# Reordering the chunk steps of a fused RWKV and expert-routing layer: the shared down projection moves one step later

## The reference

```python
# RWKV block, on layernorm(x)
xn = layer_norm(x, ln1_g, ln1_b); xx = token_shift(xn)
k, v, r = three mixes of xn and xx, times Wk, Wv, Wr
x2 = x + (sigmoid(r) * wkv(time_decay, time_first, k, v)) @ Wo.T    # wkv: a scan over the tokens
xn2 = layer_norm(x2, ln2_g, ln2_b)
kf = square(relu(mix_k(xn2) @ Wk_ffn.T))                            # 256 -> 1024
x3 = x2 + sigmoid(mix_r(xn2) @ Wr_ffn.T) * (kf @ Wv_ffn.T)
x1 = x_input + layernorm(x3)
# FFN, on xf = layernorm(x1)
shared = (gelu(xf @ w1s) * (xf @ w2s)) @ w3s                        # every token
e = argmax(xf @ Wg)
routed = (gelu(xf @ W1[e]) * (xf @ W2[e])) @ W3[e]                  # the token's own expert
out = x1 + layernorm(shared + routed)
```

## Time and profile before

| | |
|---|---|
| median of 3 runs | 1040.57 us (1040.02 to 1044.66) |
| the profiled execution | 1038.19 us, span of the core 1036.5 us |
| granted TensorE clock, mean over the span | 0.976 of full speed |
| busy in the span: PE | 934.1 us (90%), 9734 matmuls |
| busy: DVE | 760.0 us (73%) |
| busy: ACT, POOL | 589.9 us (57%), 591.9 us (57%) |
| first phase | to about 700 us |
| one turn of the loop (two steps) | 78.45 us |

### The profile page before, as it was taken

How to read it: one execution, slowest core, us unless ns; L and a number is a source line. 1 busy time by engine, 2 the same in 40 slices (tenths; PEclk the granted TensorE clock), 3 DMA queues, 4 the chain that set the end, 5 groups by cost and what they waited for, 6 DMA issues and landing times.

```text
span 1036.5 us, 28181 instructions
## 1 busy us (share of the span) xinstructions
PE 934.1 (90%) x9734; PEld 834.5 (81%) x9734; DVE 760.0 (73%) x1665; ACT 589.9 (57%) x1014; POOL 591.9 (57%) x802
## 2 busy tenths in 40 slices
PE   2388899999999999999999998879999999999994
PEld 1266788788788788888888887758999999999994
DVE  6989999999999999999999986433444444444442
ACT  5477678678678687687687675423333333333331
POOL 6346577577577577577587543234454554555553
PEclk9698999999999999999999999999999999999998
DMA  6113241341341441441443134766877788485510
GB/s 233 61 52 96 111 151 58 137 155 53 129 162 47 136 162 41 142 162 41 142 162 123 56 150 161 249 231 216 266 228 241 249 269 267 146 290 184 193 55 22
DMA packets 87330, 156.26 MB, mean 151 GB/s; under 512 B 5549, under 2 KB 68142, under 8 KB 82160
## 3 DMA queue, kind: packets, MB, share of 16 engines
q1 hardware_dynamic: 35760, 72.74, 20.5%
q10 hardware_dynamic: 46960, 65.89, 19.6%
q0 software_dynamic: 4560, 16.98, 4.3%
HBM read 178.35 MB, written 50.51 MB: 221 GB/s over the span
## 4 chain that ended last, share of the span: by engine, by line
PE 46%; DVE 18%; issue 10%; POOL 9%; ACT 7%; DMA 1%; ACTq 1%; DVEq 0%; POOLq 0%
PE up L334 9%; PE up L335 9%; PE up L336 9%; PE yp L334 4%; PE yp L335 4%; PE yp L336 4%; PE yp L538 2%; PE yp L541 2%; DVE mixed L988 2%; ACT ex L699 2%; POOL inv L1448 2%; DVE gu L1181 2%; DVE er L1058 1%; DVE arena L963 1%; POOL sh_s L1529 1%
## 5 line engine op out<-in xcount | busy, mean ns | idle before, releaser
L334 PE MATMUL up<-mix_s,arena 128*128 128x128 f16 x1248 | 211.1, 219 | 1.5 <-DMA arena<-w_split 1.5
L335 PE MATMUL up<-mix_s,arena 128*128 128x128 f16 x1248 | 211.1, 219 | 0.0
L336 PE MATMUL up<-mix_s,arena 128*128 128x128 f16 x1248 | 211.1, 219 | 0.0
L1529 POOL TENSOR_TENSOR sh_s<-gu,sh_s 128x512 f16<-128x512 f32 x64 | 84.1, 1316 | 141.5 <-ACT sh_s L762 141.5
L334 PE MATMUL up<-xf_s,arena 128*128 128x256 f16 x512 | 139.5, 272 | 1.1 <-DVE gu L1181 1.1
L336 PE MATMUL up<-xf_s,arena 128*128 128x256 f16 x512 | 139.5, 273 | 0.0
L335 PE MATMUL up<-xf_s,arena 128*128 128x256 f16 x512 | 139.5, 272 | 0.0
L1634 POOL TENSOR_TENSOR kf_s<-ex,kf_s 128x512 f16<-128x512 f32 x78 | 90.2, 1157 | 85.4 <-ACT kf_s L922 85.3
L1401 DVE SCALAR_TENSOR_TENSOR ex<-up,ex 128x512 f32<-128x512 f32 x78 | 54.0, 692 | 101.6 <-ACT ex L916 101.2
L334 PEld LDWEIGHTS up<-mix_s,arena 128*128 128x128 f16 x1248 | 122.1, 98 | 2.0 <-DMA arena<-w_split 1.7
L335 PEld LDWEIGHTS up<-mix_s,arena 128*128 128x128 f16 x1248 | 122.1, 98 | 0.4
(11 more groups left out here) (228 smaller groups left out, 2932.1 us busy)
## 6 DMA issues: line engine op xcount, KB each, us to landing
arena<-w_split ACTq DMA_DIRECT2D x117, 1024.0 KB
arena<-in_W SPq DMA_DIRECT2D x24, 1024.0 KB, 7.4
w_split<-arena SPq DMA_DIRECT2D x24, 1024.0 KB, 9.0
rows<-routed_rows ACTq DMA_DIRECT2D x39, 261.0 KB, 2.9
routed_rows<-x_in SPq DMA_DIRECT2D x8, 650.0 KB, 8.3
normed<-routed_rows ACTq DMA_DIRECT2D x39, 128.0 KB, 2.5
x_in<-in_x SPq DMA_DIRECT2D x16, 256.0 KB, 2.8
x_res<-in_x SPq DMA_DIRECT2D x16, 256.0 KB, 2.7
```

The lines of the kernel that those rows point to most:

```text
L334: pe.matmul(out, stat(0), mov(0), start=first, stop=False)
L335: pe.matmul(out, stat(0), mov(1), start=False, stop=False)
L336: return pe.matmul(out, stat(1), mov(0), start=False, stop=last)
L1529: pool.tensor_tensor(sh_s[:, 1, 2 * g:2 * g + 2, :], gu[g % GUS][:], sh_s[:, 0, 2 * g:2 * g + 2, :], ALU.subtract).then_inc(S("sh_lo"), 1)
```

## The change

The end of a chunk's work is cut off its step and put into the next one. The whole of `shared_down` of a chunk now runs one step later (chunk c3 = i-3), in pieces: q = 0 to 3 for the first 128 tokens, behind `projection(2)`, then `transpose_xf`, then q = 4 for the other 128 tokens. `ranks` also moves to c3, behind the second layer norm's transposes. The three projections stand together, and the PE step now ends with `channel_mix_down` (all four in a row), `output`, and the shared gate and up products 2 and 3. All four `channel_mix_up` stand in a row.

On DVE, `placing` moves to the next step behind the running maximum, `carry` is split from it and moved up, `scan_b` and `scan_a` now follow `kept`, both ahead of `shared(0)` and `shared(1)`; `late_lo` moves to the following step, ahead of `kept`; `gate` moves ahead of the divide; `shared(2)` and `shared(3)` stand around `x1_sum`. On ACT, `xf` and `y_shared` move into the next step, `ln0(i + 1)` moves ahead of `exps(1)` and of the gelus, and `early_hi` moves between the mixes. On POOL, the scatter moves to c3 behind `delta_of`, and `sh_lo(2)` and `sh_lo(3)` stand at the end, around `inverse3`. On SP, the store of the late piece follows in the next step, and the zeros behind the tokens are written in step 16, ahead of its stores. Seven steps are written out ahead of the loop instead of five, and the loop has four turns. The last two steps keep an order of their own and do the remaining `shared_down`. No operation of the data path is added or removed.

```diff
 PE
                 projection(0)
+                projection(1)
                 transpose_normed2()
+                ranks(before)
+                projection(2)
+                shared_down(before, 0)
+                shared_down(before, 1)
+                shared_down(before, 2)
+                shared_down(before, 3)
                 transpose_xf()
-                projection(1)
-                projection(2)
-                gate()
-                shared_gate(0)
+                shared_down(before, 4)
...
+                    shared_gate(0)
+                    gate()
+                shared_up(0)
                 shared_gate(1)
-                shared_up(0)
+                receptance()
                 shared_up(1)
-                receptance()
-                channel_mix_up(0)
-                channel_mix_up(1)
                 transpose_next()
-                channel_mix_up(2)
+                for q in range(4):
+                    channel_mix_up(q)
...
+                for q in range(4):
+                    channel_mix_down(q)
+                output()
+                shared_gate(2)
+                shared_up(2)
+                shared_gate(3)
+                shared_up(3)
 ACT
+                value()
+                if not at_step(i, NC + 1):
+                    xf(c2, p)
+                above(0)
                 xf_hi()
-                above(0)
-                value()
-                exps(0)
-                receptance()
                 above(1)
                 mix2_hi(1)
                 mix2_hi(0)
+                exps(0)
+                receptance()
+                if not at_step(i, -1):
+                    ln0(i + 1, 1 - p)
                 exps(1)
                 own(1)
                 gelu(0)
                 gelu(1)
-                if not at_step(i, -1):
-                    ln0(i + 1, 1 - p)
 DVE
                 if on(i + 1) and not at_step(i, -1):
                     ln0_moments(i + 1)
-                xf_lo()
                 if on(c1):
                     mix2(c1, 1 - p)
+                xf_lo()
...
-                if on(c0):
-                    scan_b(c0)
-                if not at_step(i, NC + 1):
+                else:
                     early_lo(i, p, h)
                 if on(c1):
                     mix2_lo(c1, 1)
                     mix2_lo(c1, 0)
+                late_lo(last_late(i, p, h))
                 if on(c0):
                     kept(c0)
-                    den_old(c0)
+                    scan_b(c0)
+                    scan_a(c0)
                 shared(0)
                 shared(1)
                 if on(c0):
+                    den_old(c0)
+                    num_old(c0)
                     den_now(c0)
 POOL
+                delta_of()
+                scatter(c3, 1 - p)
                 scatter_expert_input()
                 sh_lo(0)
-                delta_of()
-                sh_lo(1)
...
+                sh_lo(1)
+                inverse2()
+                offset2()
                 inverse1()
                 mix_lo(2)
+                sh_lo(2)
+                inverse3()
+                sh_lo(3)
```

More of the change, by code:

```diff
@@ L227, in chunk_steps @@
         def chunk_steps(eng, step):
-            turns = (NC - 4) // 2 - 1
-            for i in range(-1, 4):
+            turns = (NC - 6) // 2 - 1
+            for i in range(-1, 6):
                 step(i, i % 2, i // 2)
             with eng.Fori(0, turns) as turn:
-                step(2 * turn + 4, 0, turn + 2)
-                step(2 * turn + 5, 1, turn + 2)
-            for i in range(4 + 2 * turns, NC + 2):
+                step(2 * turn + 6, 0, turn + 3)
+                step(2 * turn + 7, 1, turn + 3)
+            for i in range(6 + 2 * turns, NC + 2):
                 step(i, i % 2, i // 2)
@@ L556, in output, with shared_down @@
                     m.then_inc(S("wo_mm"), 1)
-                def shared_down():
-                    if not on(c2):
+                def shared_down(c, q):
+                    if not on(c):
                         return
-                    if at_step(i, 2):
+                    if at_step(c, 0) and q == 0:
                         pe.wait_ge(S("piece_lo"), N_OWN)
-                    wait(pe, S("x3a"), c1 + 1 if on(c1) else NC)
-                    token_major(yp[1], sh_s, lambda s, k: shared_w[:, 2, s, k * C:(k + 1) * C], FT, "sh_dn_mm",
-                                lambda g: wait(pe, S("sh_lo"), PAIRS * c2 + g + 1))
+                    if q == 0:
+                        wait(pe, S("x3a"), c + 2 if not at_step(c, NC - 1) else NC)
+                    if q < PAIRS:
+                        wait(pe, S("sh_lo"), PAIRS * c + q + 1)
+                    for f in (2 * q, 2 * q + 1) if q < PAIRS else range(FT):
+                        t = q // PAIRS
+                        m = three(pe, yp[1][:, t, :], lambda s: sh_s[:, s, f, t * P:(t + 1) * P],
+                                  lambda s: shared_w[:, 2, s, f * C:(f + 1) * C], f == 0, f == FT - 1)
+                    if q == PAIRS:
+                        m.then_inc(S("sh_dn_mm"), 1)
@@ L607, in step @@
                     slot_step(-1, 1, -1)
-                shared_down()
+                if at_step(i, NC) or at_step(i, NC + 1):
+                    for q in range(PAIRS + 1):
+                        shared_down(c2, q)
             chunk_steps(pe, step)
@@ L1196, in early_lo, with late_lo @@
                         expert_lo(e, m)
-                def late_lo():
-                    for e, m in late_piece(i, p, h):
+                def late_lo(pieces):
+                    for e, m in pieces:
                         expert_lo(e, m)
@@ L1249, in step @@
                     halo(xnT, i + 1, 1 - p, "halo", "xnT")
+                if on(c2) and not at_step(i, NC + 1):
+                    gate(c2)
                 if on(c0):
+                    den_r(c0)
+                    num(c0)
                     divide(c0)
-                if at_step(i, NC):
-                    gate(c2)
-                    late_lo()
-                    x3_gate(c1)
-                    x3_sum(c1)
-                    x3_moments(c1)
-                shared(2)
-                if on(c0):
-                    num(c0)
+                late_lo(late_now(i, p, h))
                 if on(i + 1):
@@ L1266, in step @@
                     mix0(i + 1, 1 - p, 1)
-                if on(c2) and not at_step(i, NC) and not at_step(i, NC + 1):
-                    gate(c2)
-                if not at_step(i, NC):
-                    late_lo()
+                if on(c1):
+                    x3_gate(c1)
+                if on(i + 1):
+                    carry(i + 1)
+                if on(c1):
+                    x3_sum(c1)
                 if on(i + 1):
@@ L1273, in step @@
                 own(1)
-                if on(c1) and not at_step(i, NC):
-                    x3_gate(c1)
-                    x3_sum(c1)
-                if at_step(i, NC):
-                    x1_sum(c1, 1 - p, h + p - 1)
-                    x1_moments(c1, 1 - p)
-                shared(3)
                 if on(c0):
                     x2_sum(c0, p)
-                if on(c1) and not at_step(i, NC):
+                if on(c1):
                     x3_moments(c1)
@@ L1286, in step @@
                     x2_moments(c0)
+                shared(2)
+                if on(c1):
+                    x1_sum(c1, 1 - p, h + p - 1)
+                    if at_step(i, NC):
+                        x1_moments(c1, 1 - p)
+                shared(3)
                 if on(c1) and not at_step(i, NC):
-                    x1_sum(c1, 1 - p, h + p - 1)
                     x1_moments(c1, 1 - p)
-                if on(c2) and not at_step(i, NC + 1):
+                if at_step(i, NC):
                     placing(c2, p, h - 1)
-                if at_step(i, NC - 1):
-                    zeros_after()
                 if on(c1):
```

165 lines of the change are left out of this document (74 added, 91 removed).

## The result

The changed kernel takes 1046.11 us in the median (1042.67 to 1053.93) and the kernel before, run beside it on the same chip, 1040.36 us (1037.97 to 1044.7). The ratio is 1.0063, with a 95% interval from 1.0043 to 1.0083: slower by 0.6%. The profiled execution of the changed kernel has a span of 1042.5 us, against 1036.5.

What follows compares the result with a forecast made beforehand. PE was taken as nearly full, 37.4 us a step without waits, with DVE nearly the same floor. 12 steps x 0.7 gave +8, ends +0.4: 1038.2 became 1046.6, 1049 as a median, written as 1048; range 1016 to 1064.

Steps and rivals of the forecast that it cites:

- the case named the likeliest: Loop: the first gelu waits for inverse0 on POOL, held by DVE; 39.9 us a step against 39.22; chance 0.56.
- the ends: Steps 2 and 16: shared_down moves from one to the other, -2.5 and +2.9; together +0.4 us, bounds -3 and +4.
- The old waits: PE in the loop: waits of 2.6 us for xf and 1.0 us for sh_s a turn would both go.
- the sum: Loop durations added from x2_sum on, through DVE, POOL, ACT and PE: 38.8 us without late_lo, 41.0 with it.
- the release: Loop: time POOL needs to finish inverse0 once DVE lets it in, 0.8 or 2.1 us; 1.5 taken.
- not let in at the three boundaries in both steps: Loop before the change: POOL's inverse0 operation stays shut out between early_lo, mix2_lo, kept and one more DVE operation.
- The first rival: Loop: POOL gets in behind early_lo and PE is the bound, 37.4 us a step, 1019 us; chance 0.32.
- the upper bound: Likeliest case at its slowest: release 2.7, lag 2.7, 1 us more from DMA or collisions; 41.5 us a step, 1068 us.
- the lag: Loop: DVE reaches x2_sum late, behind x3_gate, x3_sum and mix0(2); 1.7 to 2.7 us, 2.0 taken.
- weighed `early_hi` against the loads in the loop: ACT in the loop: early_hi comes some 13 us after ln0 releases the loads; nothing counted, bound 0 to 2 us.
- The rival of bunched transfers: Four transfers at once in each second step hold early_hi, delaying mix_hi(1) and gelu(2); +18 us, 1066; chance 0.05.

Runs made afterwards that it cites:

- The two experiments on `ln0`: ln0(i + 1) moved back behind gelu(1) in the changed kernel, 1030.0 us; ln0(i + 1) alone moved ahead of exps(1) and the gelus in the kernel before, 1113.42 us.
- the two kernels with all remedies: Changed kernel with the DVE memset, ln0 behind gelu(1) and step 16's early_hi late, 1027.58 us; the same with late_lo behind the scans too, 1024.16 us.

## Why the prediction was right, and where its steps were not

The sign was right, and the mechanism in the loop was the one that the case named the likeliest gave. That the number came so near, 1048 forecast and 1046.1 measured, was luck: the loop was to cost 8 us and gained 2.4, the ends were to cost 0.4 and cost 8.4, and the two errors nearly cancelled.

**What held.** The old waits for `xf` and `sh_s` went. PE waits for the gelu instead, more with `late_lo`. DVE stands idle 2.21 us ahead of `shared(0)`. The held operation is there with 3.49 and 5.69 us. From `x2_sum` (433.93) to the end of `kept` (453.0) it is 19.1 us in the step with `late_lo`; the sum said 16.9 and 2.2, also 19.1. The release cost 0.8, the lower end of 0.8 to 2.1: POOL stood at the later of the two lines when DVE let it in. The two experiments on `ln0` show that its place is what makes the lock costly.

**The term that was mis-sized in the loop.** The steps with `late_lo` were given 41.0 us and take 41.1 in the mean from step 7 on. But the sum treated PE's wait as the whole price, 3.6 us; measured, the wait is 2.3, and in three of the four steps the matmuls behind it take 1.3 to 1.7 longer at the lower clock. The one step without the fall takes 40.47. The other step was given 38.8 and takes 38.0, with 0.4 us of wait for the gelu instead of 1.4 and no fall of the clock: the release (1.5 taken, 0.8 measured) is that difference. So the loop in its settled pattern is at 39.55, not at 39.9. This is 2.8 of the 10.7 us by which steps 3 to 14 (12 steps of 39.9 forecast, 468.1 in all measured) came out shorter.

**The step that failed: "not let in at the three boundaries in both steps".** It was read as a law from the loop before, and it holds in step 4 and from step 7 on, but not in steps 3, 5 and 6. There the first rival was the case: POOL came in at the end of `early_lo`, as the Trainium skill has it (SBUF — State Buffer, "Who interferes with whom": the blocked one gets in when the first finishes). By line 1479, 1.68 to 1.78 us in those steps, this case's trace agrees with the page there; with 3.49 and 5.69 elsewhere it does not. Steps 3 to 6 (the held step 4 among them) took 151.7 us where the sum had 159.6, which is 7.9 of the 10.7. The first rival's price was right for one kind of step: it said 37.4 us, and the kernel with the memset runs at 37.5 without `late_lo` and at 38.7 with it. There DVE, which the rival's sum left out, has 37.5 us of work; that this is the whole of the excess is my reading. Its total of 1019 was too low by that and by the ends; 1030 was measured.

**Two slips of the working.** Rows 3 and 4 show four boundaries that let nothing in, not three, since `mix2_lo` is two operations; POOL comes in behind the fifth operation, `den_old`. And the upper bound does not add up: 39.9 with 1.2 more for the release, 0.7 for the lag and 1 for DMA is 42.8 us a step, not 41.5, so about 1084 us and not 1068. Nothing that was measured hangs on it.

**The ends: +0.4 predicted, +8.4 measured.** Step 16 was right: +2.9 predicted, and from transposes to transposes it takes 42.0 instead of 39.1 us, 5.0 more of busy PE and 2.1 less of idle time. That hides a change of the order: PE's wait for `sh_s`, 2.0 us before, is 3.7 us now, since `early_hi` waits for its store ahead of the gelus. The clock falls behind it, but did so before too. The prediction weighed `early_hi` against the loads in the loop, where nothing came of it, and passed over step 16, where SP's zeros stand ahead of the stores; it named the move of the zeros nowhere. Step 15 costs 1.3 more: PE waits 2.4 us there for the second layer norm, 0.6 before, and 1.7 for `shared` on DVE. Step 17 costs 0.8 more, and 0.9 lie in the slots, which I can't account for. And step 2 was given -2.5 for its 48 matmuls less, where the fill as a whole came out at +2.6. The memset points to the lock in 1.5 of it (step 3 starts at 125.46 instead of 127.00; an operation of 4.16 us becomes one of 2.35, and PE's wait for the gelu in step 2 goes from 1.5 to 0.4). But that start lies between 125.4 and 127.3 in all the other kernels made from the changed one, with the memset or without, so it is not shown. PE's longest wait in step 2 is now 4.5 us, for which the profile names nothing; it was 1.5. That was not tried; step 2 begins 3.7 us later than before (78.88 instead of 75.18), so it stands ahead of the steps that I had looked at.

**The rival of bunched transfers** had no case in the loop: over the turn from 437.34 PE's waits name nothing that stands behind `early_hi`.

## What to carry to other kernels

Before you put work of one engine's chain in front of another engine's critical row, look up the worst single operation of that chain in the trace, not its sum: nine tiny operations of 0.2 to 0.9 us had one of 5.7 among them, since DVE's neighbours held it. A tiny operation on DVE between long ones with two inputs in SBUF, or a scan moved there, may let POOL in (the memset cost nothing here, the scan 0.5 us a step); try it where a short POOL operation is long in the trace. And price a wait of TensorE with what follows it: read the granted clock in the windows behind the wait. Here a wait of 2.29 us made the step up to 0.9 us longer on top, in some steps and not in others.

## What the runs showed of the hardware that I had not expected

- POOL's operation on two numbers per partition, reading SBUF, was held through up to five DVE operations in a row (5.69 us). It was not let in between any two of them, and ended 0.05 us after the last one. With a memset of 0.06 us and its wait, or a scan, between the first and the second it came in there, in every step. In other steps with the same DVE row it came in without either. The 20 executions of the changed kernel are spread over 11 us (1042.67 to 1053.93), the five of each of the two kernels with all remedies over less than 3.
- A scan with two inputs in SBUF holds POOL too, but each one let POOL in behind itself: line 1481 and line 1483 above last 0.52 and 0.68 us instead of 0.19, and each ends within 0.02 us of the end of a scan of 0.72 to 0.74 us. This is not peculiar to scans. In steps 3, 5 and 6, once POOL had been let in, the same two lines lasted 0.53 and 0.64 us beside the two `mix2_lo`.
- A wait of TensorE of 2.29 us in front of its matmuls was followed by a granted clock of 0.50 in three steps of the changed kernel (in the one shown from within the wait until 2.7 us behind it) and by 1.00 in the fourth. With the fall the 48 matmuls took 6.69 to 7.07 us instead of 5.40, and the step was 0.7 to 0.9 us longer. In other places a wait of 2.0 us was followed by the fall in two kernels and not in two others.
